# A 4x4 blur on one Trainium2 core: from 16 shifted taps to a product over pixels with a banded table, with the next statistics taken inside it

## The reference

```
def _gn(v, G=32, eps=1e-5):
    g = v.reshape(B_, G, C_ // G, H_, W_)
    m = jnp.mean(g, axis=(2, 3, 4), keepdims=True)
    s = jnp.var(g, axis=(2, 3, 4), keepdims=True)
    return ((g - m) / jnp.sqrt(s + eps)).reshape(v.shape)

# blur: every channel alone, 16 taps, padded by 2 before and 1 behind in both directions
xp = jnp.pad(x, ((0, 0), (0, 0), (2, 1), (2, 1)))
k = jnp.flip(kernel)[None, None, :, :]
out = jax.lax.conv_general_dilated(xr, k, window_strides=(1, 1), padding='VALID', ...)

x = x + local_attention(_gn(x))
x = x + blur(_gn(x), kernel)
x = x + global_attention(_gn(x))
x = x + spline_attention(_gn(x))
```

## Time and profile before

| | us |
|---|---|
| median of 3 runs | 7218.05 (7216.67 to 7221.30) |
| the profiled execution, its own time | 7220.95 |
| the profiled execution, its span | 7219.2 |
| blur stage and statistics "2", of the span | from 681.4 to 859 |
| busy time over the span: PE, PEld | 6310.0 (87%), 4194.2 (58%) |
| busy time over the span: DVE, ACT, POOL | 6185.6 (86%), 5681.5 (79%), 5403.4 (75%) |

### The profile page before, as it was taken

The page is one execution under the profiler, slowest core; times in us unless marked ns, Lnnn a source line. Parts: engine busy times, 40 slices in busy tenths (PEclk is TensorE's granted clock), DMA queues, the critical chain, the costliest instruction groups (busy, mean ns, idle before and its releaser), DMA issues. The chain is left out here.

```text
span 7219.2 us, 136085 instructions
## 1 busy us (share of the span) xinstructions
PE 6310.0 (87%) x37974; PEld 4194.2 (58%) x37974; DVE 6185.6 (86%) x9455; ACT 5681.5 (79%) x8932; POOL 5403.4 (75%) x3378
## 2 busy tenths in 40 slices
PE   6777899996888888888888888888888888888888
PEld 4545477674455555555555555555555555555556
DVE  4445754453999999999999999999999999999998
ACT  5371033232899999999999999999999999999997
POOL 4361000000999999999999999999999999999997
PEclk9787999998999999999999999999999999999998
DMA  3221000001000000000000000100000000000000
GB/s 96 66 70 42 0 0 0 1 0 64 11 1 1 1 1 1 1 2 11 1 1 1 1 1 2 29 1 1 1 1 1 1 2 2 4 4 4 4 4 6
DMA packets 110735, 79.83 MB, mean 11 GB/s; under 512 B 68490, under 2 KB 108290, under 8 KB 109826
## 3 DMA queue, kind: packets, MB, share of 16 engines
q1 hardware_dynamic: 107306, 77.71, 3.7%
q10 hardware_dynamic: 3288, 0.33, 0.0%
HBM read 48.70 MB, written 22.86 MB: 10 GB/s over the span
## 5 line engine op out<-in xcount | busy, mean ns | idle before, releaser
L1557 POOL TENSOR_TENSOR a_s<-a_s,a_v 128x784 f32<-128x784 f32 x1568 | 2911.5, 1857 | 319.8 <-ACT a_s L1767 308.4
L1593 PE MATMUL a_right_sides<-a_s,diag_d 128*128 128x392 f32 x6272 | 2293.6, 509 | 16.7 <-POOL a_s L1557 1.0
L1593 PEld LDWEIGHTS a_right_sides<-a_s,diag_d 128*128 128x128 f32 x6272 | 1136.6, 191 | 1070.3 <-POOL a_s L1557 333.8
L1688 DVE SCALAR_TENSOR_TENSOR a_kan<-a_s,spline_c,a_kan 128x784 f32<-128x784 f32 x1568 | 1621.4, 1034 | 51.5 <-issue 0.6
L1550 POOL TENSOR_TENSOR a_inner<-a_inner,a_x 128x784 f32<-128x784 f32 x784 | 1458.7, 1861 | 0.0
L1767 ACT ACTIVATE a_s<-a_v 128x784 f32<-128x784 f32 x1568 | 1335.4, 852 | 4.6
L1615 PEld LDWEIGHTS a_weighed<-a_V,a_probT 128*128 128x128 f32 x9800 | 1241.4, 193 | 162.2
L1758 ACT ACTIVATE a_v<-a_a 128x784 f32<-128x784 f32 x1568 | 1335.0, 852 | 0.3
L1615 PE MATMUL a_weighed<-a_V,a_probT 128*128 128x65 f32 x9800 | 1231.9, 270 | 0.0
L1605 PE MATMUL a_turned<-ident,a_prob 128*128 128x128 f32 x4900 | 798.2, 281 | 320.9 <-ACT a_probT L1775 319.3
L1580 PE MATMUL a_scores<-a_K,a_q 32*64 32x392 f32 x6272 | 701.8, 517 | 276.6 <-DVE a_kan L1670 245.4
(11 more groups left out here) (192 smaller groups left out, 5469.2 us busy)
## 6 DMA issues: line engine op xcount, KB each, us to landing
rows<-bias_rows_dram SPq DMA_DIRECT2D x112, 91.0 KB
ve<-v_dram SPq DMA_DIRECT2D x98, 104.0 KB
X<-in_x_dram SPq DMA_DIRECT2D x4, 1568.0 KB, 13.7
xn<-kt SPq DMA_DIRECT2D x56, 112.0 KB, 2.2
v_dram<-vt SPq DMA_DIRECT2D x56, 112.0 KB, 2.0
a_q<-q_dram SPq DMA_DIRECT2D x392, 16.0 KB, 2.0
mask<-in_window_mask_dram SPq DMA_DIRECT2D x56, 98.0 KB, 1.9
a_V<-v_dram SPq DMA_DIRECT2D x4, 812.5 KB, 8.6
```

Source lines behind the costliest of these rows:

```text
L1557: eng.tensor_tensor(s, s, v, ALU.mult).then_inc(cubed, 1)
L1593: mm = eng.matmul(up[:, j, 0:SUB], steps[i][:, :], cubes[g][:, SUB * j:SUB * (j + 1)], start=(i == 0), stop=(i == 1))
L1688: eng.scalar_tensor_tensor(F, banked((s1, s2)[j][g][:, :]), c[:, 3 + j:4 + j], F, ALU.mult, ALU.add).then_inc(left_added, 1)
```

## The change

Three parts.

The blur is computed with the pixels as the contracted dimension. A chunk of 448 pixels is normalised by ScalarE into `blur_xn` (L922), TensorE turns it in four pieces of 112 pixels, two image rows each (L938), ScalarE copies the four turned pieces out of PSUM into `blur_xT` (L929), and TensorE multiplies pieces of two rows (112 pixels x 128 channels, the stationary operand) with a window of a banded table `blur_band` (112 pixels x up to 8 output rows of 56, L949). The sum over six pieces gives all 16 taps of a chunk: its own four and the neighbour on either side. VectorE adds the sums to X (L966).

The `bn_stats` of each chunk for statistics "2" stand in the same loop, one chunk behind the addition (L970), and `group_norm_stats` "2" starts at `bn_aggr`.

The table is made in the `opening`: GpSimd makes a shifted unit matrix and clears the table, and VectorE adds the 16 taps one by one (L338), between the statistics of unit 0 and those of unit 1. For that the taps are the first transfer behind those of the bias table.

```
@@ -161,12 +165,15 @@
-        opening(nc, m, locals(), bias_dram)
-        for b in range(B):
-            attention0(nc, m, b, mask_dram, bias_dram)
-        group_norm_stats(nc, m, "1")
-        blur1(nc, m)
-        group_norm_stats(nc, m, "2")
+        with ExitStack() as early:
+            m.band = early.enter_context(nc.sbuf_tensor("blur_band", [TILE, BAND_ROWS * IMG], F32))
+            opening(nc, m, locals(), bias_dram)
+            for b in range(B):
+                attention0(nc, m, b, mask_dram, bias_dram)
+            group_norm_stats(nc, m, "1")
+            stats2 = early.enter_context(nc.sbuf_tensor("blur_stats", [P, UNITS, CHUNKS, 6], F32))
+            blur1(nc, m, stats2)
+            group_norm_stats(nc, m, "2", stats2)
...
@@ -218,7 +227,6 @@
-                          (m.fir[:, :], a["fir"].rearrange("a b -> (a b)").partition_broadcast(P)),
@@ -233,12 +241,14 @@
+                act.dma_start(m.fir[:, :], a["fir"].rearrange("a b -> (a b)").partition_broadcast(P)).then_inc(fir_loaded, 16)
+                act.wait_ge(fir_loaded, 16)
@@ -257,8 +267,14 @@
+                pool.memset(shift[:, :], 0.0).then_inc(shift_made, 1)
+                pool.memset(m.band[:, :], 0.0).then_inc(shift_made, 1)
+                pool.wait_ge(shift_made, 2)
+                pool.affine_select(out=shift[:, :], in_=shift[:, :], compare_op=ALU.not_equal, fill=1.0, base=-2,
+                                   pattern=[[1, TILE + KW]], channel_multiplier=-1).then_inc(shift_made, 1)
+                pool.wait_ge(shift_made, 3)
@@ -309,6 +325,19 @@
+                    if u == 1:
+                        dve.wait_ge(fir_loaded, 16)
+                        dve.wait_ge(shift_made, 3)
+                        for n, (dy, dx) in enumerate((dy, dx) for dy in range(KW) for dx in range(KW)):
+                            if n:
+                                dve.wait_ge(tap_placed, n)
+                            t = (KW - 1 - dy) * KW + KW - 1 - dx
+                            cols = slice(max(0, 2 - dx), IMG - max(0, dx - 2))
+                            pick = lambda at: at.rearrange("p (r c) -> p r c", c=IMG)[:, :, cols]
+                            band = pick(m.band[:, IMG * (4 - dy):IMG * (6 - dy)])
+                            dve.scalar_tensor_tensor(band, pick(shift[:, dx:dx + TILE]), m.fir[0:TILE, t:t + 1], band,
+                                                     ALU.mult, ALU.add).then_inc(tap_placed, 1)
+                        dve.wait_ge(tap_placed, KW * KW)
@@ -365,10 +394,11 @@
-                for u in range(UNITS):
-                    for k in range(CHUNKS):
-                        link(dve.bn_stats(stats[:, u, k, :], m.X[:, u, CHUNK * k:CHUNK * (k + 1)]))
-                dve.wait_ge(chain, done[0])
+                if counted is None:
+                    for u in range(UNITS):
+                        for k in range(CHUNKS):
+                            link(dve.bn_stats(stats[:, u, k, :], m.X[:, u, CHUNK * k:CHUNK * (k + 1)]))
+                    dve.wait_ge(chain, done[0])
@@ -868,70 +898,77 @@
-def blur1(nc, m):
...
+def blur1(nc, m, stats):
+    NORMED, KEPT, SUMS, TURNED = 4, 6, 4, 3
+    JOBS = UNITS * CHUNKS
+        xn = [st.enter_context(nc.sbuf_tensor(f"blur_xn{r}", [P, CHUNK], F32)) for r in range(NORMED)]
+        xT = [st.enter_context(nc.sbuf_tensor(f"blur_xT{r}", [TILE, 4, P], F32)) for r in range(KEPT)]
+        tp = [st.enter_context(nc.psum_tensor(f"blur_turned{r}", [TILE, 4, P], F32)) for r in range(TURNED)]
+        sums = [st.enter_context(nc.psum_tensor(f"blur_sums{r}", [P, 512], F32)) for r in range(SUMS)]
+        normed, turned, kept, summed, added, counted = (
+            sem(n) for n in ("normed", "turned", "kept", "summed", "added", "counted"))
+                for n in range(JOBS + 1):
+                    if n < JOBS:
+                        u, k = n // CHUNKS, n % CHUNKS
+                        if n >= NORMED:
+                            act.wait_ge(turned, n - NORMED + 1)
+                        act.activation(xn[n % NORMED][:, :], m.X[:, u, CHUNK * k:CHUNK * (k + 1)], ACT.Identity,
+                                       bias=m.nbias[:, u:u + 1], scale=m.rstd[:, u:u + 1]).then_inc(normed, 1)
+                    if n >= 1:
+                        c = n - 1
+                        act.wait_ge(turned, c + 1)
+                        if c >= KEPT:
+                            act.wait_ge(summed, c - KEPT + 2)
+                        act.copy(xT[c % KEPT][:, :, :], tp[c % TURNED][:, :, :]).then_inc(kept, 1)
+                def turn(n):
+                    pe.wait_ge(normed, n + 1)
+                    if n >= TURNED:
+                        pe.wait_ge(kept, n - TURNED + 1)
+                    for j in range(4):
+                        mm = pe.transpose(tp[n % TURNED][:, j, :], xn[n % NORMED][:, TILE * j:TILE * (j + 1)], m.ident[:, :])
+                    mm.then_inc(turned, 1)
+                def sum_taps(n):
+                    k = n % CHUNKS
+                    tiles = [1] + ([-1] if k else []) + [0, 2, 3] + ([4] if k < CHUNKS - 1 else [])
+                    pe.wait_ge(kept, n + 1 + (k < CHUNKS - 1))
+                    if n >= SUMS:
+                        pe.wait_ge(added, n - SUMS + 1)
+                    for t in tiles:
+                        low, high = (0, 8) if t == 1 else (max(0, 2 * t - 1), min(8, 2 * t + 4))
+                        mm = pe.matmul(sums[n % SUMS][:, IMG * low:IMG * high], xT[(n + t // 4) % KEPT][:, t % 4, :],
+                                       m.band[:, IMG * (low + 2 - 2 * t):IMG * (high + 2 - 2 * t)], start=(t == 1), stop=(t == tiles[-1]))
+                    mm.then_inc(summed, 1)
+                turn(0)
+                turn(1)
+                for n in range(JOBS):
+                    if n + 2 < JOBS:
+                        turn(n + 2)
+                    sum_taps(n)
+                for n in range(JOBS + 1):
+                    if n < JOBS:
+                        X = m.X[:, n // CHUNKS, CHUNK * (n % CHUNKS):CHUNK * (n % CHUNKS + 1)]
+                        dve.wait_ge(summed, n + 1)
+                        dve.tensor_tensor(X, X, sums[n % SUMS][:, 0:CHUNK], ALU.add).then_inc(added, 1)
+                    if n >= 1:
+                        u, k = (n - 1) // CHUNKS, (n - 1) % CHUNKS
+                        dve.wait_ge(added, n)
+                        dve.bn_stats(stats[:, u, k, :], m.X[:, u, CHUNK * k:CHUNK * (k + 1)]).then_inc(counted, 1)
+                dve.wait_ge(counted, JOBS)
```

More of the change, by code:

```diff
@@ L51 @@
 CORNER_PIX = (0, 48 * IMG + 1, 7 * IMG + 6, 55 * IMG + 7)
+KW = 4
+BAND_ROWS = 8
 HEADS3 = 4
@@ L341, in _, with group_norm_stats @@
                 dve.wait_ge(w_copied, W_BLOCKS // 4)
-def group_norm_stats(nc, m, tag):
+def group_norm_stats(nc, m, tag, counted=None):
     with ExitStack() as st:
@@ L348, in group_norm_stats @@
         sb = lambda name, shape: st.enter_context(nc.sbuf_tensor(name + tag, shape, F32))
-        stats = sb("stats", [P, UNITS, CHUNKS, 6])
+        stats = counted if counted is not None else sb("stats", [P, UNITS, CHUNKS, 6])
         sq = sb("sq", [P, UNITS])
@@ L886, in blur1 @@
         with nc.Block() as block:
[L887 to L890, removed]
             @block.scalar
             def _(act):
[L894 to L897, removed]
-                    act.activation(pad[u % 2][:, PAD:PAD + IMG, PAD:PAD + IMG], m.X[:, u, :].rearrange("p (r c) -> p r c", c=IMG),
-                                   ACT.Identity, bias=m.nbias[:, u:u + 1], scale=m.rstd[:, u:u + 1]).then_inc(padded, 1)
+                for n in range(JOBS + 1):
[11 more added lines that the diff above has]
+                        act.copy(xT[c % KEPT][:, :, :], tp[c % TURNED][:, :, :]).then_inc(kept, 1)
@@ L901, in _ @@
             @block.tensor
             def _(pe):
-                pe.wait_ge(diag_ready, TAPS_PE)
-                for u in range(UNITS):
-                    pe.wait_ge(padded, u + 1)
-                    for k in range(CHUNKS):
-                        if u:
-                            pe.wait_ge(added, CHUNKS * (u - 1) + k + 1)
-                        for j, (a, b) in enumerate(places[:TAPS_PE]):
-                            mm = pe.matmul(sums[k][:, 0:CHUNK], diag[j][:, :], pad[u % 2][:, a + 8 * k:a + 8 * (k + 1), b:b + IMG],
-                                           start=(j == 0), stop=(j == TAPS_PE - 1))
-                        mm.then_inc(pe_summed, 1)
+                def turn(n):
[5 more added lines that the diff above has]
+                    mm.then_inc(turned, 1)
@@ L914, in _ @@
+                turn(0)
[4 more added lines that the diff above has]
+                    sum_taps(n)
             @block.vector
             def _(dve):
-                for j, (a, b) in enumerate(places[:TAPS_PE]):
-                    t = tap(a, b)
-                    dve.tensor_scalar(diag[j][:, :], m.ident[:, :], m.fir[:, t:t + 1], None, ALU.mult).then_inc(diag_ready, 1)
```

(18 more changed lines are left out.)

12 lines of the change are left out of this document (2 added, 10 removed).

## The result

The changed kernel takes 7101.66 us (median of 4 runs, 7098.18 to 7109.38), the kernel before beside it 7219.68 (4 runs, 7216.67 to 7224.47): a ratio of 0.9837 [0.9820, 0.9854], 118.0 us less. The forecast was 7128 us, with 7119 to 7143 as the range, so the change gave 28 us more than forecast. The profiled execution after has a span of 7107.3 us, 111.9 less than before. Ratios go by undisturbed runs alone; one of the four runs of e8, 8042 us at a lower clock, is left out.

The account below looks back on a forecast made before the run. TensorE and VectorE, both full in the blur, were taken as the bound. The profiled 7220.95 us less 90.0 gave 7130.9; with the median of runs 2.9 lower, 7128 us, range 7119 to 7143.

Parts of the forecast that it names:

- The blur stage: Blur, entered at 681.45 us: first `bn_aggr` at 764.8 instead of 854.76, a gain of 90.0 us.
- first sum: Start of the blur: first sum on TensorE at about 685.4 us, after two chunks are normalised, turned and copied.
- TensorE's list: Blur: 28 chunks of 2.77 or 2.55 us, 75.8 us for 149.6 before, with ScalarE and VectorE hidden behind it.
- the rivals: Blur: half clock 7202 us (4%), open weight loads 7176 (6%), waiting for copies 7150 (4%), passes not overlapping 7283 (2%).
- open weight loads: Rival, blur: each of 432 TensorE passes pays 0.111 us beside its columns, 48 us more, 7176 us; chance 6%.
- passes one by one: Rival, blur: TensorE passes do not overlap at all, 432 x 0.36 = 155 us more, 7283 us; chance 2%.
- 4.1 was taken: Start of the blur: TensorE's first 4.1 us do half their work before the clock rises, 2.05 us lost.
- The statistics inside: Blur loop: `bn_stats`, 14.85 us alone before, hidden behind TensorE except at the end, where two cost 1.06 us.
- The opening: Opening: table done at 28.2 us, moments at 41.0, before TensorE takes them at 41.70; table costed at nothing.
- the cover of 0.7 us: Opening: slack between the moments at 41.0 us and TensorE being free for them at 41.70.
- The range: Whole kernel: forecast's own range 7121 to 7138 us; 7119 to 7143 for 8 times in 10.
- every later stage shifted and not changed: Stages behind the blur: a sign of being right, that they only start earlier; no term in the sum.

Follow-up runs that it names:

- e8: Changed kernel plus 13 extra VectorE multiplications of 3136 columns at the end of the blur; 7173.96 us (three runs), ratio 0.9933.
- e2: The changed kernel once more, unedited, for a second trace; 7101.9 us, ratio 0.9834.
- e4: Changed kernel with the statistics "2" taken behind the blur again, 28 in a row; 7114.95 us, ratio 0.9854.
- e1: The kernel before once more, unedited, for a second trace; 7221.68 us, ratio 1.0002.
- e5: Kernel before with five extra, unread TensorE products in each tile of the last attention; 7195.86 us, ratio 0.9960.
- e6: Changed kernel with five extra, unread TensorE products in each tile of the last attention; 7111.82 us, ratio 0.9847.
- e9: Changed kernel plus 31 VectorE instructions of 4 columns at the end of the blur, giving the count of before, 2798; 7136.14 us, ratio 0.9888.
- e10: Kernel before plus 224 VectorE semaphore increments in the opening; 7205.87 us, ratio 0.9988.
- e7: Changed kernel plus 26 VectorE instructions of 4 columns at the end of the blur; 7125.15 us, ratio 0.9863.
- e3: Changed kernel plus 26 VectorE multiplications over a whole unit, about 91 us, at the end of the blur; 7209.05 us, ratio 0.9983.
- e11: Changed kernel plus 256 VectorE semaphore increments in the opening; 7118.09 us, ratio 0.9862.

## Why the prediction was wrong

- *The blur stage: right.* 83.05 us from entry to first `bn_aggr`, 83.3 forecast. Chunk 2.72 us for 2.77; first sum 4.14 us after the entry, 4.0 forecast. That TensorE's list is the only bound held. None of the rivals came: the products waited 0.0 us for anything, the clock was 1.00 from 690 us on, and 432 passes in 78.97 us, 0.18 us each, leave no room for open weight loads or for passes one by one. That the gain came out to 0.25 us is partly luck: the chunks were some 1.2 us cheaper over the list, and the clock, 0.50 up to 688.3 us or 5.5 us of products where 4.1 was taken, cost 0.7 more; in e2 the same stretch takes 82.05 us. ScalarE's normalising was mis-sized (0.76 us a chunk for 0.63) and stayed hidden.
- *The statistics inside: right*, by e4 (13.05 us).
- *The opening: right, and in part by luck.* The table ended at 28.43 (28.2 forecast): the steps took 0.37 us instead of 0.32, but the taps let them start at 22.57 and not 23.1. The moments came 0.6 us ahead of their product; the cover of 0.7 us was thin, and held.
- *The range.* By its own terms the lower end is 7122.5 and not 7121; that changes nothing.
- *The step that failed* is the last one: "every later stage shifted and not changed", priced at nothing in the sum and in the range. The later stages became 19.0 us shorter in the profiles shown, 28.9 in e1 and e2. With 90.25 and 2.7 the 19.0 make the 111.9 us of the spans. Filled (e5, e6), the later stages differ by 3.8 us the other way, and the two kernels by 84.0 us, which is near the 90 forecast.
- *What stood in its place*: the change takes 32 instructions out of VectorE's list ahead of the last attention (2798 to 2766). A gap of 0.1 us in every second tile of the second pair goes away (e9 puts it back, e10 takes it out of the kernel before); by itself that is some 2 us. The rest goes with the clock of TensorE: it falls at fewer places, and the last 38 us no longer run at half clock. The gain beyond 90 is luck: e7, with 26 small instructions more, loses 16.8 us of it, and e9, with the count of before, 18.7.
- *What stays open.* That the loops' place in VectorE's list makes the gap, because VectorE waits there for its own instructions, is an inference; no row names what the gap waits for. The Trainium skill (Runtime: NRT & Kernel Launch, Instruction fetch mechanics) says that instructions come in blocks of 256 and that a taken branch out of the two blocks held has to wait for a fetch; the runs agree as far as 256 more changed nothing in the pattern. How the small losses lead to a fall of the clock is not shown either: in all tiles of 30.18 us the fall begins 0.3 to 0.5 us behind a tile's reciprocal, so it may be the moment in a tile that decides. The end points the same way: where it is slow (before, e1, e3, e7, e9, e10) the clock falls 7.5 to 8.3 us behind the third last reciprocal and stays down to the end, and where it is fast (after, e2, e4, e8, e11) it falls 0.0 to 0.3 us ahead of that reciprocal, is back 3.4 us later, and falls again only behind the last one. Whether the end falls cannot be told from the losses alone: e10 and e11 have the same ones, and another end. The edit also changes the lists of TensorE, ScalarE and GpSimd; no run changes those alone.

## What to carry to other kernels

A stage whose engines' lists are counted from rows can be forecast to a microsecond or two, and here it was. But this kernel, with long loops in which TensorE now and then falls to half clock, has a spread of some 20 to 30 us (0.4%) that edits ahead of the loops win or lose: 26 or 31 small instructions were enough, and 8.9 us differ between two executions of one kernel. In such a kernel put it into the range on both sides, and before a gain of that size is credited to an edit, look at the stages that it didn't touch, and try it with a few instructions of padding. Where the clock is the carrier, a little useless work for TensorE can make a kernel faster (e5), but need not (e6).

## What was not expected of the hardware

- Extra work made a kernel faster: 0.9960 [0.9946, 0.9975] for five unread products a tile in the kernel before.
- An instruction list that is longer by 26 tiny instructions (e7) changed tile times 1060 us later, and the end, 6300 us later; the later stages took 16.8 us more.
- A `sem_inc` on VectorE is no cheap filler: 256 of them took 20.86 us, and delayed the first `bn_aggr` by 12.0 us, though VectorE had 8.82 us of waiting there to spare.
- Transposes do not keep the clock down here: with 112 of 432 passes being transposes, the granted clock was 1.00 in the windows from 690 and from 700 us. The Trainium skill (TensorE: Matmul & The Clock Gate, Part 4: PE-mode transpose) says that full clock does not engage for transposes; for such a mixture the measurement decides. No run here has transposes alone.
- A `bn_stats` of 448 columns lasts 0.62 us here and lasted 0.615 before (median at L370), but in a row the next starts after 0.53 us: the price of one in a row is not what one takes alone.
